# Graph attention done densely: a new order of heads over three PSUM banks, the next block's levels one product at a time, a target row in three bf16 parts, and totals in a bank of their own

## What is computed

```python
def _gat_layer(h, src, dst, Ws, Wd, a_s, a_d, bias):
    xs = (h @ Ws).reshape(N, H, C)
    xd = (h @ Wd).reshape(N, H, C)
    alpha_s = jnp.sum(xs * a_s, axis=-1)
    alpha_d = jnp.sum(xd * a_d, axis=-1)
    e = jax.nn.leaky_relu(alpha_s[src] + alpha_d[dst], 0.2)
    emax = jax.ops.segment_max(e, dst, num_segments=N)
    ex = jnp.exp(e - emax[dst])
    denom = jax.ops.segment_sum(ex, dst, num_segments=N)
    alpha = ex / (denom[dst] + 1e-16)
    msg = xs[src] * alpha[:, :, None]
    return jax.ops.segment_sum(msg, dst, num_segments=N).reshape(N, H * C) + bias
for i in range(3):
    h = _gat_layer(h, src, dst, Ws[i], Wd[i], att_s[i], att_d[i], b[i])
    if i < 2: h = jax.nn.relu(h)
```

## Time and profile before

| | us |
|---|---|
| median of 3 runs (5263.87 to 5265.28) | 5264.95 |
| the profiled execution's own time | 5259.3 |
| its span in the trace | 5257.5 |
| dense attention, first weigh to last reciprocal (893.0 to 3836.2) | 2943.2 |
| the rest (edges, other three layers) | 2314.3 |

### The profile page before, as it was taken

The page is one execution under the profiler, slowest core; times in us unless marked ns, Lnnn a source line. Parts: engine busy times, 40 slices in busy tenths (PEclk is TensorE's granted clock), DMA queues, the critical chain, the costliest instruction groups (busy, mean ns, idle before and its releaser), DMA issues.

```text
span 5257.5 us, 59119 instructions
## 1 busy us (share of the span) xinstructions
PE 3943.7 (75%) x16302; PEld 1689.8 (32%) x16302; DVE 3670.2 (70%) x8162; ACT 3263.5 (62%) x7606; POOL 1873.8 (36%) x1368
## 2 busy tenths in 40 slices
PE   6999796666666666666666666666669999986899
PEld 3444344111111121111112111111137667654444
DVE  8999784777777757777775777777767777774311
ACT  5888404777667756777775777777757667674100
POOL 0000131444333323333332434444437777773000
PEclk9999896676766666666666676766679999997899
DMA  4444642111111101111111111111026776763566
GB/s 154 157 154 155 228 167 72 39 39 58 39 39 39 60 19 40 39 39 60 40 39 39 40 39 39 39 39 58 0 85 231 239 240 232 241 217 105 183 229 224
DMA packets 387474, 552.25 MB, mean 105 GB/s; under 512 B 23781, under 2 KB 358021, under 8 KB 386922
## 3 DMA queue, kind: packets, MB, share of 16 engines
q1 hardware_dynamic: 358114, 494.48, 27.1%
q0 software_dynamic: 23024, 48.93, 3.4%
q10 hardware_dynamic: 6040, 5.35, 0.4%
HBM read 352.81 MB, written 195.86 MB: 104 GB/s over the span
## 4 chain that ended last, share of the span: by engine, by line
DVE 34%; ACT 19%; PE 17%; issue 11%; DMA 6%; POOL 3%; SPq 2%; ACTq 0%; DVEq 0%; POOLq 0%
DVE pick L1861 12%; PE quad L1109 7%; ACT quad L891 7%; DVE big L1861 6%; ACT pick L879 6%; DVE big L1853 6%; DMA src_bc<-pe_src_d 3%; POOL big L736 2%; PE psS L1230 2%; DMA big<-table_d,src_win 2%; DVE big L1982 2%; PE psZ L1302 2%; PE quad L1430 1%; DVE sm L1885 1%; ACT hT L977 1%
## 5 line engine op out<-in xcount | busy, mean ns | idle before, releaser
L719 POOL TENSOR_TENSOR pick<-pick,big 128x800 f32<-128x800 f32 x600 | 1131.4, 1886 | 1913.7 <-ACT pick L879 1913.7
L891 ACT ACTIVATE quad<-big,keep 128x400 f32<-128x400 f32 x1200 | 705.8, 588 | 770.1 <-DVE big L1861 770.1
L1302 PE MATMUL psZ<-big 128*64 128x400 f32 x2400 | 799.3, 758 | 469.6 <-DVE big L1861 468.2
L1302 PE MATMUL psL<-pick,big 128*64 128x400 f32 x2400 | 794.5, 754 | 207.2 <-DVE pick L1861 206.4
L1861 DVE SCALAR_TENSOR_TENSOR pick<-quad,big 128x400 f32<-128x400 f32 x1200 | 650.0, 572 | 303.3 <-ACT quad L891 302.7
L1861 DVE SCALAR_TENSOR_TENSOR big<-quad,big 128x400 f32<-128x400 f32 x1200 | 682.4, 569 | 113.1 <-ACT quad L891 113.1
L736 POOL DMA_INDIRECT big<-table_d,src_win x672 | 645.4, 960 | 279.5 <-issue 189.3
L879 ACT ACTIVATE pick<-big,keep 128x400 f32<-128x400 f32 x1200 | 735.0, 613 | 0.5
L891 ACT ACTIVATE quad<-pick,keep 128x400 f32<-128x400 f32 x1200 | 659.1, 579 | 3.1 <-POOL pick L719 3.1
L1302 PEld LDWEIGHTS psZ<-big 128*64 128x64 f32 x2400 | 161.2, 179 | 1066.9 <-DVE big L1861 1042.2
L1982 DVE SCALAR_TENSOR_TENSOR big<-big,keep_win,quad 128x256 f32<-128x256 f32 x784 | 375.8, 479 | 152.0 <-ACT quad L1010 81.6
(11 more groups left out here) (361 smaller groups left out, 6474.5 us busy)
## 6 DMA issues: line engine op xcount, KB each, us to landing
big<-A_d SPq DMA_DIRECT2D x17, 6400.0 KB
rows_d<-big SPq DMA_DIRECT2D x112, 896.0 KB
A_d<-big SPq DMA_DIRECT2D x396, 200.0 KB, 1.9
big<-A_d SPq DMA_DIRECT2D x24, 2600.0 KB, 9.9
big<-A_d SPq DMA_DIRECT2D x24, 2400.0 KB, 9.4
big<-A_d SPq DMA_DIRECT2D x32, 1600.0 KB, 11.0
big<-table_d,src_win POOLq DMA_INDIRECT x672
src_bc<-pe_src_d SPq DMA_DIRECT2D x56, 64.0 KB
```

The costliest lines, as they stand in the source:

```text
L719: pool.tensor_tensor(soft_2[n % A_SLOTS], soft_2[n % A_SLOTS], row_2[J % 2], ALU.add).then_inc(bent_p, 1)
L891: nc.scalar.activation(psE[h], soft(n, h), ACT.Exp, bias=s_all[:, 2, n % NT, h:h + 1]).then_inc(soft_rdy, 1)
L1302: ins = nc.tensor.matmul(acc[a][64 * k:64 * k + 64, 0:CH], xs_1[:, t, a, C * k:C * k + 2 * C], soft(n, 2 * a + k), start=False, stop=(t == ...
```

## The change

Scores and weights are the same numbers up to rounding. In words:

- The three banks rotate over all exponentials (`bank`), the order of the heads is 3, 0, 1, 2 on ACT and DVE, and the half bends stand between them, two tiles ahead for head 0 and one for head 1. `bend` for head 2 moves into its own tile.
- The sums are eight products with 32 stationary columns each: numerators of the four heads into the four quarters of `acc[0]`, totals (ones) into those of `acc[1]`. All stand behind the last weigh of the tile.
- ACT copies both banks out whole (two instructions in tile 1), so PE waits for `totals_rdy` and not for the division; `divide` moves to the end of tile 3 with one multiplication, `layer_rows` to tile 6.
- `own_rows` goes to tile 1 of PE, its copy (`own_row`) to tile 3 of ACT. The 25 level products are spread: one behind each of tiles 3 to 15, six behind tiles 16 and 17. `highest` goes to tile 18, `top` becomes a part of `near` in tile 19.
- The target row is cut into three bf16 parts on partitions 0, 32 and 64 (`cut_row` on DVE, four instructions; `middle_part` on ACT), and spread by one bf16 product of 96 rows in place of the fp32 one. Rows 0 to 2 are spread behind tiles 20 to 22, row 3 and the two `keep_row` behind tile 23, and the last two copies stand at the end of ACT's tile 23.
- Features go to SBUF in one copy per tile and not in two; the row scale 0.2 moves into the constants.

```diff
+        BANK_ORDER = (3, 0, 1, 2)
+        EXP_AT = (2, 3, 4, 1)
+        WEIGH_AT = (2, 3, 4, 1)
+        def bank(n, h):
+            return psW[(H * n + BANK_ORDER.index(h)) % len(psW)]
+        def bank_free(n, h):
+            at = H * n + BANK_ORDER.index(h) - len(psW)
+            return H * (at // H) + WEIGH_AT[BANK_ORDER[at % H]] if at >= 0 else 0
...
+            def own_row(J):
+                act.wait_ge(lev_ps, 3 * J + 1)
+                nc.scalar.mul(own_4, psR[0:H, :], NEG_SLOPE).then_inc(lead_rdy, 1)
+            def middle_part(J):
+                act.wait_ge(near_rdy, 2 * J + 2)
+                nc.scalar.copy(parts[J % 2][32:32 + H, :], mid_4).then_inc(lead_rdy, 1)
...
             def totals(J):
                 act.wait_ge(summed, NT * (J + 1))
-                for h in range(H):
-                    total = (C, 2 * C)[h % 2]
-                    ins = nc.scalar.copy(share[C * h:C * h + C, :], acc[h // 2][total:total + C, 0:CH])
-                ins.then_inc(totals_rdy, 1)
+                if J:
+                    act.wait_ge(share_rdy, J)
+                nc.scalar.copy(share, acc[0][:, 0:CH])
+                nc.scalar.copy(total_b, acc[1][:, 0:CH]).then_inc(totals_rdy, 1)
...
                     for t in range(NT):
                         n = NT * J + t
-                        exponent(n, 0)
-                        exponent(n, 1)
-                        exponent(n, 2)
-                        if ahead:
-                            half_bend(n + 2, 0)
-                        exponent(n, 3)
-                        if ahead:
-                            half_bend(n + 2, 1)
-                        if c and t == 0:
+                        exponent(n, 3)
+                        if left > 2:
+                            half_bend(n + 2, 0)
+                        exponent(n, 0)
+                        if left > 1:
+                            half_bend(n + 1, 1)
+                        exponent(n, 1)
+                        exponent(n, 2)
+                        if c and t == 1:
                             totals(J - 1)
-                        if c and t == 2:
+                        if c and t == 6:
                             layer_rows(g, J - 1)
-                        if c < NCH - 1 and 19 <= t < 19 + H:
-                            near_row(J + 1, t - 19)
+                        if c < NCH - 1:
+                            if t == 3:
+                                own_row(J + 1)
+                            if t == 20:
+                                middle_part(J + 1)
+                            if t == 21 or t == 22:
+                                near_row(J + 1, t - 21)
+                            if t == 23:
+                                near_row(J + 1, 2)
+                                near_row(J + 1, 3)
...
+            def weighted_sums(n):
+                J, t = n // NT, n % NT
+                if t == 0:
                     if J:
+                        pe.wait_ge(totals_rdy, J)
+                    nc.tensor.matmul(acc[1][:, 0:CH], of_eps[0:1, :], ones_row[0:1, :], start=True, stop=False)
+                pe.wait_ge(weight_rdy, H * n + H)
+                for h in range(H):
+                    nc.tensor.matmul(acc[0][C * h:C * h + C, 0:CH], xs_1[:, t, C * h:C * h + C], soft(n, h),
+                                     start=(t == 0), stop=(t == NT - 1))
+                for h in range(H):
+                    ins = nc.tensor.matmul(acc[1][C * h:C * h + C, 0:CH], ones[:, 0:C], soft(n, h), start=False, stop=(t == NT - 1))
+                ins.then_inc(summed, 1)
...
                     for t in range(NT):
                         n = NT * J + t
+                        weighted_sums(n)
                         if c < NCH - 1:
-                            if t == 16:
-                                levels(g, J + 1)
+                            if t == 1:
+                                own_rows(g, J + 1)
+                            if 3 <= t < 16:
+                                levels(g, J + 1, t - 3, t - 2)
+                            if t == 16 or t == 17:
+                                levels(g, J + 1, SPLIT + 6 * (t - 16), SPLIT + 6 * (t - 15))
+                            if t == 18:
+                                top_rows(J + 1)
+                            if 20 <= t < 23:
+                                spread_row(J + 1, t - 20)
+                            if t == 23:
+                                spread_row(J + 1, 3)
+                                keep_row(J + 1, 1)
+                                keep_row(J + 1, 0)
...
+            def cut_row(J):
+                high = parts[J % 2][0:H, :]
+                link(v.tensor_copy(high, v_4))
+                link(v.tensor_tensor(m_4, v_4, high, ALU.subtract))
+                link(v.tensor_copy(mid_4, m_4))
+                v.tensor_tensor(parts[J % 2][64:64 + H, :], m_4, mid_4, ALU.subtract).then_inc(near_rdy, 1)
...
+            def divide(J):
+                dve.wait_ge(totals_rdy, J + 1)
+                link(v.reciprocal(total_b, total_b))
+                v.tensor_tensor(share, share, total_b, ALU.mult).then_inc(share_rdy, 1)
...
-                weigh(n, 0)
-                weigh(n, 1)
-                if bends:
-                    bend(n + 1, 0)
-                weigh(n, 2)
-                if bends:
-                    bend(n + 1, 1)
-                weigh(n, 3)
+                weigh(n, 3)
+                bend(n, 0)
+                weigh(n, 0)
+                if left > 1:
+                    bend(n + 1, 1)
+                weigh(n, 1)
+                weigh(n, 2)
...
                     for t in range(NT):
                         n = NT * J + t
-                        tile_weights(n, t < NT - 1 or c < NCH - 1)
+                        tile_weights(n, NT * (NCH - c) - t)
+                        if c and t == 3:
+                            divide(J - 1)
                         if c < NCH - 1:
-                            if t == 16:
+                            if t == 18:
                                 highest(J + 1)
-                            if t == 17:
-                                top(J + 1)
-                            if t == 18:
+                            if t == 19:
                                 near(J + 1)
-                        if c and t == 0:
-                            divide(J - 1)
+                                cut_row(J + 1)
```

More of the change, by code:

```diff
@@ L218, in build @@
         psN = [psL, psZ]
-        psE = [quad[:, 512 * i:512 * i + CH] for i in (0, 1, 2, 2)]
+        psW = [quad[:, 512 * i:512 * i + CH] for i in range(3)]
         psV = [quad[:, 3 * 512:3 * 512 + CH], psH[:, 0:CH]]
@@ L899, in _ @@
                     act.wait_ge(xs_ps, NT * g + t + 1)
-                    for k in range(2):
-                        ins = nc.scalar.copy(xs_1[:, t, :, 2 * C * k:2 * C * k + C],
-                                             psY[t % 2][:, 0:D].rearrange("p (a h c) -> p h a c", a=2, h=2)[:, k, :, :])
-                    ins.then_inc(xs_rdy, 1)
+                    nc.scalar.copy(xs_1[:, t, :], psY[t % 2][:, 0:D]).then_inc(xs_rdy, 1)
                 act.wait_ge(lev_rdy, 2 * g + 1)
@@ L1218, in _, with own_rows @@
             pe.wait_ge(node_out, NT)
-            def levels(g, J):
-                for late in range(2):
-                    k = 2 * J + late
-                    pe.wait_ge(a_part[k % RING], 16 * (k // RING + 2))
-                pe.wait_ge(lev_rdy, 2 * g + 2)
+            def own_rows(g, J):
                 if J:
                     pe.wait_ge(row_rdy, H * J)
-                for t in range(NT):
+                nc.tensor.matmul(psR[0:H, :], w_att[:, g, D + H:D + 2 * H], feat[g % 2][:, CH * (J % NCH):CH * (J % NCH + 1)],
+                                 start=True, stop=True).then_inc(lev_ps, 1)
@@ L1230, in levels @@
+            def levels(g, J, first, last):
+                if first == 0:
+                    pe.wait_ge(lead_rdy, 2 * J + 1)
+                for t in range(first, last):
+                    if t == 0 or t == SPLIT:
+                        k = 2 * J + (t == SPLIT)
+                        pe.wait_ge(a_part[k % RING], 16 * (k // RING + 2))
                     ins = nc.tensor.matmul(psR.rearrange("l (b w) -> l b w", w=W), lev[:, t, :, :].rearrange("p h k -> p (h k)"),
                                            marks_of(J, t), start=(t == 0), stop=(t == NT - 1))
-                ins.then_inc(lev_ps, 1)
+                if last == NT:
+                    ins.then_inc(lev_ps, 1)
@@ L1880, in tile_weights @@
                     dve.sem_inc(ring_used, 1)
-            def divide(J):
-                dve.wait_ge(totals_rdy, J + 1)
-                link(v.reciprocal(share, share))
-                for h in range(H):
-                    own = (0, 3 * C)[h % 2]
-                    v.tensor_tensor(share[C * h:C * h + C, :], acc[h // 2][own:own + C, 0:CH], share[C * h:C * h + C, :],
```

(4 more changed lines are left out.)

167 lines of the change are left out of this document (73 added, 94 removed).

## The result

The changed kernel takes 4754.26 us (median of 4 runs, 4748.57 to 4758.67) against 5264.41 for the kernel before beside it (5263.04 to 5265.28): a ratio of 0.9031, interval 0.9015 to 0.9046, faster by 510 us. The prediction was 4800 with a range from 4680 to 4945.

A forecast was written before the change was run, and what follows sets the result against it. No engine was always busy; a shared-bank stall in each tile and the work between blocks set the time. 5265 - 426 (plain tiles) - 19 (changes of block) - 20 (layer starts and ends) = 4800 us, range 4680 to 4945.

The forecast's parts named there:

- The plain tile: A tile of dense attention without block-change work falls from 3.87 to 3.16 us, 426 us less over 600 tiles.
- the loop through POOL's add: Half bend of head 1, POOL's add, ACT's exponential, next half bend: 3.16 us per tile, just above ACT's 3.12.
- Four products together: Four 32-column products on PE run together; a tile's two groups take 1.6 us at the higher clock, 3.0 at the lower.
- Rivals 1 and 2: PE's products run two at a time (4960 us, chance 0.11) or one after another (about 6180 us, chance 0.05).
- The change of block: Work between blocks adds 22 us (16.4 to 29.7) over plain tiles, before 22.9; 19 us less over 21 changes.
- the division: In the change of block, DVE's reciprocal of 2.65 and one multiplication of 0.6: 2.9 to 3.25 us.
- `near` with `cut_row`: In the change of block, eight dependent DVE instructions on four partitions, ACT waiting behind them: 4.1 to 4.7 us.
- rival 3: DVE's short `cut_row` copies and the division's multiplication wait out POOL's adds: 79 us more, 4880 us, chance 0.14.
- Levels, `highest` and the rows: In the change of block: level products 0 to 3.5 us, `highest` 0.7 to 4.9, middle part and row copies 5.2 to 8.3.
- The totals: In the change of block, two ACT copies, then exponentials waiting behind a half bend for PE's sums: 2.5 to 4.0 us.
- Starts and ends: At the starts and ends of layers, 7 us less per layer (2 to 10), 20 us in all.
- Rival 4: The stall moves from head 3's bank to POOL's add, lengthened to 2.6 us: time near 5240 us, chance 0.03.

## Why the prediction held, step by step

- **The plain tile: right.** 3.16 forecast, 3.14 measured, so 600 x 0.73 = 438 where 426 was taken. The shared bank was the cause (the run with fixed banks: 3.89), and the loop through POOL's add bounds it now, 0.02 above ACT's own 3.12 (add every 3.13; 3.12 when the half bend is a tile earlier).
- **Four products together: right.** Two groups take 1.6 us at the higher clock, as worked out. Rivals 1 and 2 fall by the start times alone: four within tens of ns, no offset of 0.35 between pairs.
- **The change of block: right in the sum, with errors of both signs in it.** 20.4 for 22, so 52 us gained where 19 was forecast. Two terms came above their own range: the division 4.1 for at most 3.25, and `near` with `cut_row` 5.7 for at most 4.7. The step that failed is the price of 0.56 to 0.6 for the multiplication and the subtraction, which held only with POOL idle: under its add they took 1.67 and 2.12. That is rival 3's mechanism, which the prediction kept out of the sum. It came in part: 1.1 + 1.55 = 2.65 us a block for the 3.8 that it priced, about 56 us, and in a subtraction of two SBUF operands. The short copies that it named took 0.35, but they started only when the add was over (1055.52 after 1055.07), so no run tests them under it.
- Levels, `highest` and the rows came at their low ends: 0 for up to 3.5, 0.75 for up to 4.9, 5.5 for up to 8.3. The step that failed there is the clock: 0.68 to 0.72 was carried over from the trace of before, 2 parts in 5 at the higher level, and the stage now has 0.86, 1.00 in the plain tiles shown, 0.76 around the row. The totals still ran mostly at the lower level (0.58 in their window, passes of 0.88 where the plain tile has 0.51 to 0.53), and they came near their high end. The last tile of a block shows the same: 6.10 us in 17 of 21 changes, at 0.95 to 1.00, and 6.87 to 7.62 in the other four, at 0.50 to 0.72. No run holds the clock at the lower level, so for the levels and `highest` this cause is argued and not shown.
- **Starts and ends: right.** 20 forecast, 7 a layer; the remainder is 510 - 438 - 52 = 20. From the last weigh of a layer to the first of the next it is 61.2 us where it was 67.9, and the stage's first weigh comes 6.1 earlier.
- **Sum.** 4800 less 12 for the tile and 33 for the block gives 4755. That the middle value came within 46 us is partly luck, because the errors in the change of block run against each other: the two terms priced too low lie 1.85 above their ranges together, while the levels, `highest` and the rows lie at or near the low ends of theirs, some 10 under the high ends.
- Rival 4 did not come: POOL's add takes 1888 ns on the mean, as before, beside a DVE that is busier. (By the prediction's own terms its price was 4800 + 426 = 5226, not 5240; and the tile of 3.25 in its high end of 5030 rests on no row.)

The Trainium skill, "SBUF — State Buffer", section Who interferes with whom, has the rule that decides between the two subtractions: a DVE instruction with two SBUF inputs contends with a GpSimd instruction that reads SBUF, and whichever comes second waits out the first. The trace agrees, 2.12 us with two and 0.57 with one.

The Trainium skill, "TensorEngine Tiling (Array Packing)", section Tiling Modes, says that a change of tiling mode drains the engine. It costs nothing that a run here shows: tiles with a level product between the groups of 32 columns stay at 3.14, and with the levels spread the kernel is 62 us faster than with them in one place.

## What to carry to other kernels

When a stall that recurs in every tile goes, what hid in it comes to light: the same change of block cost 15.0 us in the slow tile and 20.4 in the fast one, so price two such edits together, not one after the other. Before moving a short DVE instruction under POOL's work, count its operands in SBUF; putting one in PSUM, or moving it into a stretch where POOL idles, took away 1.1 to 1.6 us each. Put an unavoidable wait of one engine (ACT for the totals) and an unavoidable job of another (DVE's reciprocal) in the same tile: that alone gave some 75 to 80 us here.

## What the runs showed of the hardware

- A TENSOR_TENSOR of 4 x 400 fp32 with both operands in SBUF takes 0.56 us alone and up to 2.13 when POOL's add of 128 x 800 began before it; with one in PSUM it takes 0.57 beside the add.
- A cast of 4 x 400 to bf16 takes 0.355 us from SBUF and 0.56 from PSUM.
- Products on four separate quarters of the columns start within tens of ns of one another, and the order in which the program lists them by quarter made no difference (4752.88 and 4754.26). The eight fp32 products of a tile take 1.55 us in a plain tile at a granted clock of 1.00 and 2.9 at the lower level (986.71 to 989.60).
- The granted clock of the dense stage rose from 0.68 to 0.86 while PE's busy share of it fell from 67% (1973.57 of 2943.2) to 56% (1375.72 of 2445). The trace shows both and no run here separates them: part of the shorter busy time is the clock itself.
